# A graph network on one core: 72 instead of 76 dense blocks, seven instead of six gather steps beside each

## The chip, the cores and the metric

One NeuronCore of a Trainium2 chip runs the whole program. The metric is the device time of one execution in microseconds (us). Durations come from one execution recorded by the hardware profiler.

## The reference

A graph of 12,500 nodes and 400,000 edges (sorted by destination; low node numbers have many more incoming edges) goes through two layers, with a layer norm after each. Three times the rows of a table are summed over the edges of each node.

```python
agg = segment_sum(x[src], dst, n)                       # round 1
h   = relu(concat([x, agg / max(deg, 1)]) @ W_fc + b_fc) + x @ W_res + b_res
x   = layernorm(x + h)
# general conv, twice (rounds 2 and 3)
msg = x[src] @ Wm + bm + edge_attr @ We + be
out = segment_sum(msg, dst, n) + x @ Ws + bs            # relu between the two
x   = layernorm(x + out)
```

Since the weights can be applied ahead of the sum, each round is: a table y of 12,544 rows of 64 (65 in round 1) numbers, each split into three bf16 parts; and for each node the sum of y[src] over its edges.

## The kernel before

**Two ways of summing.** Nodes stand in 98 blocks of 128. The first 76 blocks (`END`) are *dense*: a matrix of edge counts, 128 nodes by 12,544 sources in fp16, is multiplied with the whole table, 98 matmuls of 128x192 (`dense`, L1106). The matrices are made in round 1 and stored to DRAM (`a_dram`, 3.1 MB a block); rounds 2 and 3 load them again, in two halves for each of two buffers (`a_load`, L1502). Edges of later blocks, and those that the dense lists don't take, are *gathered*: a step is a tile of 128 edges whose table rows GpSimd fetches with an indirect DMA (`g_fetch`, L1262), and three matmuls with a one-hot of the destinations (`g_multiply`, L1093); VectorE adds the result to a node block (`g_add`, L791).

**Making the matrices (round 1, `r == 0`).** A block is built in windows of 4 nodes. A step takes 128 edges, VectorE makes two one-hots from comparisons (`pairs`, L801, called in L828 to L830: one over sources' high part and the window's nodes, one over the source's lane), and TensorE multiplies them into PSUM (L1132); ACT evicts two windows at once (L1398). `REGIONS` gives for the blocks from 0, 2, 8 and 30 how many nodes one step covers (1, 1, 2, 4), and `FIRST` gives for the 256 nodes of blocks 0 and 1 how many steps each node gets: eight for the first 8 nodes, four for the next 24, three for 32, two for 192. One-hots lie in a ring of 16 steps. TensorE works on the dense product of the block before between the windows of the one being built.

**The gather steps beside.** `WITH` = 38 pairs of blocks run with `G` = 6 gather steps beside each block, 456 places. ACT converts the row numbers of six steps (`g_stage`, L1375, the tile `idx`), GpSimd issues six gathers, VectorE makes six one-hots in one operation (`g_mark`, L784, the tile `hot_g`), TensorE multiplies after the block, VectorE adds. Two sets of buffers alternate (`j`): a set is free after its product (`gsum`). In rounds 2 and 3 the second half of a list waits until half of the next dense product is done. If the list is longer than the places, a loop of `more` passes follows each round (L1162 and alike).

**What is in order where.** Each engine runs its instructions in the order written; they meet through semaphores. VectorE's queue in rounds 2 and 3 is: one-hots for the block, the reduction of the block's product (L880), its addition (L885), then the additions of the gather product. GpSimd's queue holds gathers alone in the rounds; SP's queue holds the loads or stores of matrices.

**Before and between the rounds.** A setup of some 260 us finds the edges of each step (it copies a halo of `BACK` tiles, the deepest entry of the lists, in front of each lane's edges, L1440 and L1441; shifts and comparisons over it, L532 to L564) and fetches them with GpSimd's gathers (L1213). After round 1 edge features are summed (L1172 to L1181), and the tables of rounds 2 and 3 are made ahead of each.

Of the kernel before, what the change touches and what calls it, by code (L numbers as in the profile page):

```python
# [30 lines left out]
ALU = mybir.AluOpType  # L31
ACT = mybir.ActivationFunctionType
# [3 lines left out]
P = 128  # L36
EPS = 1e-5
WD = 4
N_NODES, N_EDGES = 12500, 400000
BLOCKS = -(-N_NODES // P)  # L40

REGIONS = ((0, 1, 0), (2, 1, 1), (8, 2, 1), (30, 4, 1))
FIRST = ((8, 8), (24, 4), (32, 3), (192, 2))
END = 76
WITH = 38
WPB = P // WD
# [3 lines left out]
def runs():  # L50

    found, step = [], 0
    for n, (b, wd, k) in enumerate(REGIONS):
        end = REGIONS[n + 1][0] if n + 1 < len(REGIONS) else END
        node = b * P
        for nodes, deep in ((((end - b) * P, k),) if k else FIRST):
            found.append((node, wd, nodes // wd, deep, step))
            node += nodes
            step += nodes // wd * deep
        assert node == end * P  # L60
    return found, step

def regions():

    found, (all_runs, _) = [], runs()
    for n, (b, wd, k) in enumerate(REGIONS):
        end = REGIONS[n + 1][0] if n + 1 < len(REGIONS) else END
        inside = [run for run in all_runs if b * P <= run[0] < end * P]
        deeps = [max(run for run in inside if run[0] <= node)[3] for node in range(b * P, (b + 2) * P, WD)]  # L70
        found.append((b - REGIONS[0][0], end - b, wd, (deeps[0:WPB], deeps[WPB:2 * WPB]), inside[0][4]))
    return found
# [33 lines left out]
def gnn_program(nc, step_c, first_row, x, src, dst, edge_attr, W_fc, b_fc, W_res, b_res,  # L106
                Wm1, bm1, We1, be1, Ws1, bs1, Wm2, bm2, We2, be2, Ws2, bs2, out):
    N, D = N_NODES, x.shape[0]
    E = src.shape[0]
    assert (N, E) == (N_NODES, N_EDGES)  # L110
    T = E // P
# [7 lines left out]
    HIS = BLOCKS  # L119
    WIN = HIS * WD  # L120
    HALF = HIS // 2
    G, GW = 6, 8
    GI = WITH
# [16 lines left out]
    NB = 7  # L140
# [8 lines left out]
    CW = CG * P  # L149
    spans_of = [(s0, (REG + [(0, 0, 0, 0, CW)])[n + 1][4], wd) for n, (_, _, wd, _, s0) in enumerate(REG)]  # L150
    PIECES = 16
    HB, RING = 4, 16
    AHEAD = RING - HB + 1
    at_once = lambda wd: HB if wd == WD else 2 * HB
    YW, YW0 = BLOCKS * 3 * D // 2, BLOCKS * 3 * F1 // 2
    RINGS = RING * (P + WIN) // 2
    UNION = max(2 * CW + RINGS, 3 * CW)
    PATH = ES * P + P
    SETS = SPAD // G
# [7 lines left out]
    assert UNION >= YW >= BLOCKS * D and G * F1 <= 512 and 0 < GI <= ITERS and all(b <= 2 * GI or b - n >= 2 * GI for n, b in ((r[1], r[0] + r[1]) for r in REG)) and B0 >= 0 and DB % 2 == 0 and WPB % HB == 0  # L167
    assert all(n % 2 == 0 and s0 % P == 0 and sum(d) * WD // wd % RING == 0 for _, n, wd, ds, s0 in REG for d in ds) and HIS % 2 == 0 and (SETS - SETS % 2) * G >= T + BLOCKS - 1

    ctx = ExitStack()  # L170
    with ctx:
        def sb(name, shape, dt=F32):
            return ctx.enter_context(nc.sbuf_tensor(name, shape, dt))
# [35 lines left out]
        twofold = sb("twofold", [P, D])  # L209
        idx = sb("idx", [P, 2 * G], I32)  # L210
        hot_g = sb("hot_g", [P, 2 * G, P], F16)
        part_d = sb("part_d", [P, 2, F1])
# [24 lines left out]

        KEPT = 8 * NB
        x1_head = union[:, YW:YW + KEPT * D].rearrange("p (b d) -> p b d", d=D)
# [90 lines left out]
        trB = sb("trB", [64, P], U8)[:, :]  # L330
        trF = sb("trF", [64, P])[:, :]
        mu, root, rstd = (smallf[:, k * CG:k * CG + BLOCKS] for k in (0, 4, 8))
# [145 lines left out]
        def _(dve):  # L478
# [248 lines left out]
            for r in range(3):  # L727
# [56 lines left out]
                def g_mark(it, j):  # L784
                    dve.wait_ge(gsum[r][j], it + 1)
                    V.tensor_tensor(hot_g[:, j * G:(j + 1) * G, :],  # L786
                                    code_g[:, bass.ds((it * 2 + j) * G, G)].unsqueeze(2).to_broadcast([P, G, P]),
                                    lane16[:, 0:P].unsqueeze(1).to_broadcast([P, G, P]), ALU.is_equal)\
                        .then_inc(marked[r][j], 1)
# [20 lines left out]
                if r == 0:  # L810
# [4 lines left out]

                    for b0, blocks, wd, deeps, s0 in REG:
                        upto, pair = steps_upto(wd, deeps)
                        many = at_once(wd)
                        with dve.Fori(0, blocks // 2) as i:
                            for j in range(2):  # L820
# [3 lines left out]
                                for q in range(upto[j][0], upto[j][WPB]):  # L824
                                    n, s = q % RING, bass.ds(i * pair + (q + s0), many)
                                    if q % many == 0:

                                        dve.wait_ge(stepped, i * pair + (q + s0 + many - HB + 1))  # L828
                                        pairs(hot_c[:, n:n + many, 0:HIS * wd], twice_h, s, HIS * wd)
                                        pairs(hot_c[:, n:n + many, WIN:WIN + P], twice_l, s, P).then_inc(made, many // HB)  # L830
# [153 lines left out]
        def _(pe):  # L984
# [69 lines left out]
            for r in range(3):  # L1054
# [58 lines left out]
                if r == 0:  # L1113

                    pe.wait_ge(s_v, mark["zeros"])
                    for b0, blocks, wd, deeps, s0 in REG:
                        upto, pair = steps_upto(wd, deeps)
                        many = at_once(wd)
                        with pe.Fori(0, blocks // 2) as i:
                            for j in range(2):  # L1120
                                it = i + b0 // 2
                                for q in range(upto[j][0], upto[j][WPB]):
                                    w = max(k for k in range(WPB) if upto[j][k] <= q)
                                    c, deep = q - upto[j][w], deeps[j][w]
                                    if q % many == 0:
                                        pe.wait_ge(made, i * (pair // HB) + ((q + s0 + many) // HB))
                                    if c == 0 and w % 2 == 0:
# [66 lines left out]
        def _(pool):  # L1194
# [38 lines left out]
            for r in range(3):  # L1233
# [28 lines left out]
                def g_fetch(it, j, spread=False):  # L1262
                    pool.wait_ge(staged[r][j], it + 1)
                    pool.sem_inc(claimed, 1)
                    for k in range(G):
                        if spread and k == G // 2:

                            pool.wait_ge(a_used[1 - j][0], it + (1 + (r - 1) * ITERS + j))
                            pool.sem_inc(claimed, 1)
                        s = j * G + k  # L1270
                        pool.indirect_dma_start(msg[:, s, 0:3 * width_of[r]], None, y_tab[r], bass.IndirectOffsetOnAxis(  # L1271
                            ap=idx[:, s:s + 1], axis=0)).then_inc(gathered[r][j], 16)
# [33 lines left out]
        def _(act):  # L1306
# [28 lines left out]
            for r in range(3):  # L1335
# [39 lines left out]
                def g_stage(it, j):  # L1375
                    act.wait_ge(gsum[r][j], it + 1)
                    A.activation(idx[:, j * G:(j + 1) * G], src_g[:, bass.ds((it * 2 + j) * G, G)], ACT.Copy)\  # L1377
                        .then_inc(staged[r][j], 1)

                if r:  # L1380
# [3 lines left out]
                else:  # L1384

                    act.wait_ge(ready, 1)
                    for b0, blocks, wd, deeps, s0 in REG:
                        upto, pair = steps_upto(wd, deeps)
                        with act.Fori(0, blocks // 2) as i:
                            for j in range(2):  # L1390
# [5 lines left out]
                                for w in range(0, WPB, 2):  # L1396
                                    act.wait_ge(stepped, i * pair + (upto[j][w + 2] + s0 + AHEAD))
                                    A.activation(abuf[:, j, :].rearrange("p (h w d) -> p w h d", w=WPB, d=WD)  # L1398
                                                 [:, w:w + 2, :, :],
                                                 ps[:, w % 4:w % 4 + 2, 0:WIN].rearrange("p w (h d) -> p w h d", d=WD),  # L1400
                                                 ACT.Copy).then_inc(evacd, 2)
# [33 lines left out]
        def _(sp):  # L1435
# [55 lines left out]
            for r in range(3):  # L1491
# [26 lines left out]
                if r == 0:  # L1518

                    for b0, blocks, _, _, _ in REG:  # L1520
                        with sp.Fori(0, blocks // 2) as i:
# [66 lines left out]
```

## Time and profile before

| | us |
|---|---|
| median of three runs | 3590.77 (3587.72 to 3591.53) |
| span of the profiled execution | 3585.2 |
| setup, to about | 259 |
| round 1 | 259 to 1514 |
| edge features | 1539 to 2047 |
| round 2's dense blocks | 2151 to 2818 |
| round 3's dense blocks | 2880 to 3553 |

Busy shares of the whole span: TensorE 88%, VectorE 65%, GpSimd 56%, ACT 45%. An average over such different stages says little, so every stage is read by itself: stretches (busy time of each engine between two moments), the timeline of one engine, waits (who waited for whom, summed) and groups of instructions by line. In the views PE is TensorE's matmul, PEld its weight load, DVE VectorE, ACT ScalarE, POOL GpSimd, SP SyncE. Matmuls of one line are merged in a timeline, and their listed length has the pipeline's depth in it, so it is their starts that tell the pace.

### The profile page before, as it was taken

The numbers are of one execution on the slowest core, as the hardware profiler recorded it, in microseconds if no ns is written. First come the engines' busy times: TensorE is split into PE (matmuls) and PEld (weight loads), VectorE is DVE, ScalarE is ACT, GpSimd is POOL, SyncE is SP. The second block draws the span as 40 slices with busy tenths as digits, with TensorE's granted clock in tenths as the row PEclk, the third lists the DMA queues.
The fourth block names the chain that finished last, engine by engine and source line by source line (L and its number), as shares of the span: only waits on it lengthen the run. The fifth ranks groups of instructions, "written<-read, shape, count | busy, mean of one in ns | idle before, by whom it ended". The sixth has DMA issues, their size and how long they took to land.

```text
span 3585.2 us, 114923 instructions
## 1 busy us (share of the span) xinstructions
PE 3167.6 (88%) x39408; PEld 2958.1 (83%) x39408; DVE 2339.3 (65%) x5369; ACT 1613.7 (45%) x2096; POOL 2021.8 (56%) x2292
## 2 busy tenths in 40 slices
PE   0239999999999999889999889999999889999995
PEld 0127988888888888778888879999999889999995
DVE  8779998888888888779999682333333423333335
ACT  0123677878999999788988650000000400000000
POOL 6761234445666666534444256666666666666664
PEclk9869999999999999999999979999999999999998
DMA  3521455556666666668888429999999599999996
GB/s 92 134 18 70 167 194 198 218 213 233 238 240 251 251 238 240 245 207 247 248 246 247 147 93 400 403 402 402 402 402 403 202 354 403 402 402 402 402 402 241
DMA packets 232872, 959.10 MB, mean 268 GB/s; under 512 B 44815, under 2 KB 144285, under 8 KB 173818
## 3 DMA queue, kind: packets, MB, share of 16 engines
q1 hardware_dynamic: 186027, 884.48, 65.0%
q0 software_dynamic: 46784, 73.84, 6.8%
q8 instruction: 33, 0.54, 0.1%
q14 instruction: 28, 0.23, 0.0%
HBM read 694.75 MB, written 263.40 MB: 267 GB/s over the span
## 4 chain that ended last, share of the span: by engine, by line
PE 68%; DVE 11%; issue 8%; POOL 6%; DVEq 3%; ACT 2%; DMA 2%; SPq 0%; ACTq 0%; POOLq 0%
PE ps L1109 48%; PE ps L1132 10%; DVE union L805 5%; PE ps L1179 4%; PE ps L1101 3%; POOL abuf L1213 3%; DVE union L921 2%; ACT union L1416 1%; DVE abuf L932 1%; POOL union L1213 1%; PE ps L1069 1%; DVEq L466 1%; DVEq L932 1%; PE ps L1188 1%; POOL abuf L1255 0%
## 5 line engine op out<-in xcount | busy, mean ns | idle before, releaser
L1271 POOL DMA_INDIRECT msg<-y_tab,idx x1368 | 1531.1, 1119 | 1041.9 <-ACT idx L1377 652.0
L1109 PE MATMUL ps<-union,abuf 128*128 128x192 bf16 x14896 | 1265.3, 247 | 13.9 <-DVEq L782 10.2
L1109 PEld LDWEIGHTS ps<-union,abuf 128*128 128x128 f16 x14896 | 1226.7, 98 | 21.2 <-issue 10.6
L1398 ACT ACTIVATE abuf<-ps 128x784 f16<-128x784 f32 x1216 | 1000.7, 823 | 239.9 <-PE ps L1132 212.3
L805 DVE TENSOR_TENSOR union<-lane,union 128x1568 f16<-128x1568 f16 (+3 forms) x1440 | 949.5, 710 | 31.0 <-PE ps L1132 27.1
L1109 PE MATMUL ps<-early,abuf 128*128 128x195 bf16 x7546 | 853.4, 249 | 0.0
L1109 PEld LDWEIGHTS ps<-early,abuf 128*128 128x128 f16 x7546 | 677.1, 99 | 100.9
L1132 PE MATMUL ps<-union 128*128 128x392 f16 (+2 forms) x4288 | 689.5, 288 | 52.4 <-DVE union L805 47.1
L1377 ACT ACTIVATE idx<-src_g 128x6 int32 (+1 forms) x228 | 46.4, 205 | 1280.2 <-PE ps L1101 1277.9
L1179 PE MATMUL ps<-union 128*64 128x128 f32 x7280 | 444.4, 278 | 48.2 <-ACT union L1416 48.1
L1179 PEld LDWEIGHTS ps<-union 128*64 128x64 f32 x7280 | 394.1, 137 | 98.4 <-DVE abuf L932 79.2
L1416 ACT ACTIVATE union<-union 128x1280 f32<-128x1280 f16 x364 | 432.9, 1259 | 55.9 <-DVE union L921 53.9
L797 DVE TENSOR_TENSOR acc<-acc,ps 128x64 f32 (+1 forms) x918 | 203.7, 222 | 364.2 <-DVE acc L797 211.2
L1132 PEld LDWEIGHTS ps<-union 128*128 128x128 f16 x4288 | 362.9, 108 | 92.3 <-issue 48.3
L921 DVE TENSOR_TENSOR union<-lane,rel_e 128x640 f16<-128x640 f16 x728 | 352.5, 484 | 41.7 <-issue 40.3
L1291 POOL TENSOR_TENSOR rel_e<-early,base_e 128x10 f16 x728 | 208.4, 305 | 287.5 <-DVE union L921 271.1
L880 DVE TENSOR_REDUCE part_d<-ps 128x64 f32<-128x192 f32 x152 | 54.4, 358 | 459.2 <-PE ps L1109 459.2
L786 DVE TENSOR_TENSOR hot_g<-code_g,lane 128x768 f16<-128x768 f16 x228 | 218.0, 956 | 70.2 <-DVE acc L797 69.2
L932 DVE TENSOR_TENSOR abuf<-abuf,ps 128x128 f32 x728 | 203.5, 280 | 1.8 <-PE ps L1179 1.1
L1101 PE MATMUL ps<-msg,hot_g 128*128 128x64 bf16 (+1 forms) x4104 | 167.2, 194 | 5.5 <-DMA msg<-y_tab,idx 5.5
L1101 PEld LDWEIGHTS ps<-msg,hot_g 128*128 128x128 f16 x4104 | 157.0, 98 | 6.0 <-DMA msg<-y_tab,idx 6.0
L854 DVE TENSOR_TENSOR acc<-acc,ps 128x65 f32 x456 | 99.5, 218 | 56.8 <-DVE acc L854 37.9
(229 smaller groups left out, 1241.4 us busy)
## 6 DMA issues: line engine op xcount, KB each, us to landing
abuf<-a_dram SPq DMA_DIRECT2D x304, 1568.0 KB
a_dram<-abuf SPq DMA_DIRECT2D x76, 3136.0 KB
union<-in_edge_attr_dram SPq DMA_DIRECT2D x728, 160.0 KB, 2.9
msg<-y_tab,idx POOLq DMA_INDIRECT x1368
y_tab<-union SPq DMA_DIRECT2D x28, 336.0 KB, 2.2
abuf<-in_x_dram SPq DMA_DIRECT2D x28, 224.0 KB, 3.4
y_tab<-early SPq DMA_DIRECT2D x7, 682.5 KB, 5.5
out_dram<-union SPq DMA_DIRECT2D x2, 800.0 KB, 3.5
```

The source lines that it names most:

```text
L786: V.tensor_tensor(hot_g[:, j * G:(j + 1) * G, :], code_g[:, bass.ds((it * 2 + j) * G, G)].unsqueeze(2).to_broadcast([P, G, P]), lane16[:, ...
L805: return V.tensor_tensor(to.rearrange("p s (c u) -> p s c u", u=2), lanes.unsqueeze(1).to_broadcast([P, n, width // 2, 2]), codes[:, which ...
L921: marks = V.tensor_tensor(mark_e[:, h, :, :].rearrange("p j (c u) -> p j c u", u=2), lane16[:, 0:P].rearrange("p (c u) -> p c u", u=2).uns ...
L932: V.tensor_tensor(to, to, ps[:, b, 0:P], ALU.add).then_inc(e_add, 1)
L1101: last = nc.tensor.matmul(tile_ps(r, j, k), hot_g[:, s, :], msg[:, s, c * width_of[r]:(c + 1) * width_of[r]], start=c == 0, stop=c == 2)
L1109: last = nc.tensor.matmul(ps[:, bank, 0:3 * width_of[r]], abuf[:, buffer, hi * P:(hi + 1) * P], ycols[r][:, hi, :], start=hi == 0, stop=hi ...
L1132: nc.tensor.matmul(ps[:, w % 4, 0:WIN].rearrange("p (h d) -> p h d", d=WD)[:, :, d0:d0 + wd], hot_c[:, n, WIN:WIN + P], hot_c[:, n, 0:HIS ...
L1179: last = nc.tensor.matmul(ps[half:half + D, h, 0:P], feats[:, h, j * D:(j + 1) * D], hot_e[:, h, j, :], start=j < 2, stop=j >= EG - 2)
L1271: pool.indirect_dma_start(msg[:, s, 0:3 * width_of[r]], None, y_tab[r], bass.IndirectOffsetOnAxis(ap=idx[:, s:s + 1], axis=0)).then_inc(ga ...
L1291: nc.gpsimd.tensor_tensor(rel_e[:, h, :, :], flat(dst_e[:, bass.ds(grp[h], 1), :]).unsqueeze(2) .to_broadcast([P, EG, 2]), base_e[:, bass. ...
L1398: A.activation(abuf[:, j, :].rearrange("p (h w d) -> p w h d", w=WPB, d=WD) [:, w:w + 2, :, :], ps[:, w % 4:w % 4 + 2, 0:WIN].rearrange("p ...
L1416: A.activation(hot_e[:, h:h + 2, :, :], mark_e[:, h:h + 2, :, :], ACT.Copy)\
```

## The change

Dense blocks end at 72 instead of 76, with seven gather steps beside each (504 places instead of 456). The lists of blocks 0 and 1 become 14 steps for the first 4 nodes, six for 20, three for 32, two for 200. A region's list begins at a multiple of 128 columns now (`s0`), and the count of steps before it is kept apart for the semaphores (`e0`). In rounds 2 and 3 ACT converts the destination codes of a list as well, to fp32 in a new tile `codes`, and VectorE makes each step's one-hot by itself, comparing the lanes with one number per lane; it waits for ACT's copy, and GpSimd's wait counts in twos. The scratch tile `trF` moves into `part_d`.

```diff
-FIRST = ((8, 8), (24, 4), (32, 3), (192, 2))
-END = 76
-WITH = 38
+FIRST = ((4, 14), (20, 6), (32, 3), (200, 2))
+END = 72
+WITH = 36
...
         node = b * P
+        step = -(-step // P) * P
...
-    G, GW = 6, 8
+    G, GW = 7, 8
...
+        codes = sb("codes", [P, 2 * G])
...
-        trF = sb("trF", [64, P])[:, :]
+        trF = part_d[0:64, :, :].rearrange("p j d -> p (j d)")[:, 0:P]
...
                 def g_mark(it, j):
                     dve.wait_ge(gsum[r][j], it + 1)
+                    if r:
+                        dve.wait_ge(staged[r][j], it * 2 + 2)
+                        for s in range(j * G, (j + 1) * G):
+                            last = V.tensor_scalar(hot_g[:, s, :], lane16[:, 0:P], codes[:, s:s + 1], None, ALU.is_equal)
+                        last.then_inc(marked[r][j], 1)
+                        return
...
-                                        dve.wait_ge(stepped, i * pair + (q + s0 + many - HB + 1))
+                                        dve.wait_ge(stepped, i * pair + (q + e0 + many - HB + 1))
...
                 def g_fetch(it, j, spread=False):
-                    pool.wait_ge(staged[r][j], it + 1)
+                    pool.wait_ge(staged[r][j], it * 2 + 1 if r else it + 1)
...
                     A.activation(idx[:, j * G:(j + 1) * G], src_g[:, bass.ds((it * 2 + j) * G, G)], ACT.Copy)\
                         .then_inc(staged[r][j], 1)
+                    if r:
+                        A.activation(codes[:, j * G:(j + 1) * G], code_g[:, bass.ds((it * 2 + j) * G, G)], ACT.Copy)\
+                            .then_inc(staged[r][j], 1)
```

## Rows read from the trace of the kernel before

**Rows 1.** Stretches: length, busy time (instructions) by engine, clock, DMA share, GB/s.

```profile
2151.00:2818.00 667.00, 663.83 (x8795) 660.26 (x8793) 216.14 (x676) 15.36 (x74) 453.58 (x456) 0.99 1.00 398
...
498.70:831.50 332.80, 305.45 (x3603) 282.67 (x3601) 295.72 (x500) 265.01 (x341) 151.96 (x121) 1.00 0.55 212
902.30:1475.50 573.20, 573.20 (x5922) 485.45 (x5921) 503.59 (x1000) 530.72 (x680) 357.50 (x240) 1.00 0.63 245
```

**Rows 2.** Timeline of TensorE, rounds 2 and 3: start, length, instructions, idle before.

```profile
2166.76 0.74 PE L1101 MATMUL ps<-msg,hot_g 128*128 128x64 bf16 x18 [0.30 <-DMA msg<-y_tab,idx]
...
2626.50 0.72 PE L1101 MATMUL ps<-msg,hot_g 128*128 128x64 bf16 x18
...
2635.22 0.73 PE L1101 MATMUL ps<-msg,hot_g 128*128 128x64 bf16 x18
2635.79 8.29 PE L1109 MATMUL ps<-union,abuf 128*128 128x192 bf16 x98
...
2818.13 0.72 PE L1101 MATMUL ps<-msg,hot_g 128*128 128x64 bf16 x18
...
2894.78 1.14 PE L1101 MATMUL ps<-msg,hot_g 128*128 128x64 bf16 x18 [5.25 <-DMA msg<-y_tab,idx]
...
3548.23 0.72 PE L1101 MATMUL ps<-msg,hot_g 128*128 128x64 bf16 x18
```

**Rows 3.** DMA, 2300 to 2500: packets, MB, share of 16 engines; gathers issued.

```profile
q0 software_dynamic: 4419, 6.79, 9.5%
...
msg<-y_tab,idx POOLq DMA_INDIRECT x139
```

**Rows 4.** Timeline of GpSimd and VectorE in round 2.

```profile
2160.82 0.95 POOL L1271 DMA_INDIRECT msg<-y_tab,idx  x1 [0.30 <-issue]
...
2302.13 0.96 DVE L786 TENSOR_TENSOR hot_g<-code_g,lane 128x768 f16<-128x768 f16 x1 [0.72 <-DVE acc L797]
...
2302.36 1.55 POOL L1271 DMA_INDIRECT msg<-y_tab,idx  x1 [0.30 <-issue]
...
2314.54 0.94 POOL L1271 DMA_INDIRECT msg<-y_tab,idx  x1 [1.28 <-issue]
```

**Rows 5.** The same two engines' timelines in the setup.

```profile
114.02 2.17 POOL L1213 DMA_INDIRECT union<-both_dram,gidx  x1 [0.30 <-issue]
...
114.98 1.09 DVE L611 TENSOR_SCALAR acc<-code_g,tiles 125x3328 f16<-125x3328 f16 x1
...
119.12 0.94 POOL L1213 DMA_INDIRECT union<-both_dram,gidx  x1 [0.30 <-issue]
...
119.23 0.42 DVE L623 TENSOR_SCALAR acc<-code_g,tiles 125x768 f16<-125x768 f16 x1
```

**Rows 6.** Groups, 902 to 1475: count, busy us, mean ns, idle before.

```profile
L854 DVE TENSOR_TENSOR acc<-acc,ps 128x65 f32 x240 | 52.5, 219 | 33.1 <-DVE acc L854 21.4 <-DVE acc L848 11.6
L786 DVE TENSOR_TENSOR hot_g<-code_g,lane 128x768 f16<-128x768 f16 x40 | 38.0, 951 | 0.0
```

**Rows 7.** Waits, 902 to 1475: us in total, times, longest.

```profile
DVE part_d L842 <- PE ps L1101: 21.8, 40, 0.7
...
DVE union L805 <- PE ps L1132: 13.5, 40, 0.3
```

**Rows 8.** Waits, 498 to 831.

```profile
DVE union L805 <- PE ps L1132: 10.5, 40, 0.3
DVE part_d L842 <- issue: 9.0, 20, 0.5
```

**Rows 9.** Groups, 268 to 358.

```profile
L805 DVE TENSOR_TENSOR union<-lane,union 128x1024 f16<-128x1024 f16 x78 | 53.3, 683 | 0.0
...
L805 DVE TENSOR_TENSOR union<-lane,union 128x784 f16<-128x784 f16 x78 | 43.8, 561 | 0.1
```

**Rows 10.** DMA, 0 to 20.

```profile
DMA packets 733, 4.45 MB, mean 223 GB/s; under 512 B 264, under 2 KB 264, under 8 KB 388
```

**Rows 11.** Timeline of VectorE in the setup.

```profile
22.45 2.36 DVE L532 CAST union<-abuf 125x4224 int16<-125x4224 int32 x1
```

More of the change, by code:

```diff
@@ L64, in regions @@
 def regions():
-    found, (all_runs, _) = [], runs()
+    found, (all_runs, _), before = [], runs(), 0
     for n, (b, wd, k) in enumerate(REGIONS):
@@ L70, in regions @@
         deeps = [max(run for run in inside if run[0] <= node)[3] for node in range(b * P, (b + 2) * P, WD)]
-        found.append((b - REGIONS[0][0], end - b, wd, (deeps[0:WPB], deeps[WPB:2 * WPB]), inside[0][4]))
+        found.append((b - REGIONS[0][0], end - b, wd, (deeps[0:WPB], deeps[WPB:2 * WPB]), inside[0][4], before))
+        before += sum(windows * deep for _, _, windows, deep, _ in inside)
     return found
@@ L149, in gnn_program @@
     CW = CG * P
-    spans_of = [(s0, (REG + [(0, 0, 0, 0, CW)])[n + 1][4], wd) for n, (_, _, wd, _, s0) in enumerate(REG)]
+    spans_of = [(s0, (REG + [(0, 0, 0, 0, CW)])[n + 1][4], wd) for n, (_, _, wd, _, s0, _) in enumerate(REG)]
     PIECES = 16
@@ L156, in gnn_program @@
     RINGS = RING * (P + WIN) // 2
-    UNION = max(2 * CW + RINGS, 3 * CW)
+    KEPT = 8 * NB
+    UNION = max(2 * CW + RINGS, 3 * CW, YW + KEPT * D)
     PATH = ES * P + P
@@ L167, in gnn_program @@
     assert UNION >= YW >= BLOCKS * D and G * F1 <= 512 and 0 < GI <= ITERS and all(b <= 2 * GI or b - n >= 2 * GI for n, b in ((r[1], r[0] + r[1]) for r in REG)) and B0 >= 0 and DB % 2 == 0 and WPB % HB == 0
-    assert all(n % 2 == 0 and s0 % P == 0 and sum(d) * WD // wd % RING == 0 for _, n, wd, ds, s0 in REG for d in ds) and HIS % 2 == 0 and (SETS - SETS % 2) * G >= T + BLOCKS - 1
+    assert all(n % 2 == 0 and s0 % P == 0 and sum(d) * WD // wd % RING == 0 for _, n, wd, ds, s0, _ in REG for d in ds) and HIS % 2 == 0 and (SETS - SETS % 2) * G >= T + BLOCKS - 1
     ctx = ExitStack()
@@ L236, in gnn_program @@
         hot_c = union[:, 2 * CW:2 * CW + RINGS].bitcast(F16).rearrange("p (s c) -> p s c", s=RING)
-        KEPT = 8 * NB
         x1_head = union[:, YW:YW + KEPT * D].rearrange("p (b d) -> p b d", d=D)
@@ L813, in _ @@
                     step(V.memset(ps[:, 7, :], 0.0), "zeros")
-                    for b0, blocks, wd, deeps, s0 in REG:
+                    for b0, blocks, wd, deeps, s0, e0 in REG:
                         upto, pair = steps_upto(wd, deeps)
@@ L1115, in _ @@
                     pe.wait_ge(s_v, mark["zeros"])
-                    for b0, blocks, wd, deeps, s0 in REG:
+                    for b0, blocks, wd, deeps, s0, e0 in REG:
                         upto, pair = steps_upto(wd, deeps)
@@ L1125, in _ @@
                                     if q % many == 0:
-                                        pe.wait_ge(made, i * (pair // HB) + ((q + s0 + many) // HB))
+                                        pe.wait_ge(made, i * (pair // HB) + ((q + e0 + many) // HB))
                                     if c == 0 and w % 2 == 0:
@@ L1386, in _ @@
                     act.wait_ge(ready, 1)
-                    for b0, blocks, wd, deeps, s0 in REG:
+                    for b0, blocks, wd, deeps, s0, e0 in REG:
                         upto, pair = steps_upto(wd, deeps)
@@ L1396, in _ @@
                                 for w in range(0, WPB, 2):
-                                    act.wait_ge(stepped, i * pair + (upto[j][w + 2] + s0 + AHEAD))
+                                    act.wait_ge(stepped, i * pair + (upto[j][w + 2] + e0 + AHEAD))
                                     A.activation(abuf[:, j, :].rearrange("p (h w d) -> p w h d", w=WPB, d=WD)
@@ L1518, in _ @@
                 if r == 0:
-                    for b0, blocks, _, _, _ in REG:
+                    for b0, blocks, _, _, _, _ in REG:
                         with sp.Fori(0, blocks // 2) as i:
```

## The prediction

> **What bounds the kernel now.** First the stretches by stage [rows 1]: in round 2 (2151 to 2818) TensorE is busy 663.8 of 667 us, but the DMA engines are busy throughout too, at 398 GB/s; two limits lie on top of each other. TensorE's timeline tells which one is ahead [rows 2]: a block with its gather product returns every 8.72 us late in the round (2626.50 to 2635.22), while the whole round's 75 intervals from first to last product (2166.76 to 2818.13, 651.4 us) average 8.685, so early ones are shorter (if half go at 8.72, the others go at 8.65). That is a TensorE that first outruns the transfers, uses up what was loaded ahead, and then goes at their pace: 8.72 is the DMA limit, about 8.65 TensorE's. Round 3 is alike (653.5 us). Third, GpSimd's timeline [rows 4]: a gather takes 0.94 us and 0.30 lies between two, so six need 7.5 of the 8.7 us. It waits for its index list in between, and nobody waits for it except at a round's start, where the first product stands at 2166.76 though the sixth gather was issued at 2160.82.
>
> In round 1, blocks 30 and up (40 of them from 902.3 to 1475.5, 14.33 us each) have TensorE busy 573.2 of 573.2 us [rows 1], with VectorE at 503.6. Blocks 8 to 29 (20 from 498.7 to 831.5, 16.64 us each) have TensorE at 305.4 and VectorE at 295.7 of 332.8 us: there they pass the ring of one-hots back and forth and each waits for the other. Blocks 0 to 7 go by VectorE's one-hots.
>
> **Does the work fit the loops?** A fallback loop of further gathers runs after each round if the list is longer than the steps beside the blocks. I counted the list on the reference's edges by the kernel's own rule (a tile is listed, once for each block it spans, if one of its edges is beyond the lists' depth or at a node past the last dense block): 436 of 456 places before, 496 of 504 after. Each round issues 504 gathers instead of 456, with no loop behind. Without the deeper first lists it would have been 514.
>
> **The change part by part**, in us.
>
> *Four blocks fewer in round 1:* 4 x 14.33 = -57.3.
>
> *The seventh step in round 1.* For TensorE three matmuls: eighteen take 0.57 (2635.22 to 2635.79) [rows 2], so 0.095 a block. For VectorE a sixth more one-hot (0.951 / 6 = 0.16) and one more addition (0.219, and 33.1 / 240 = 0.14 of waiting) [rows 6], together 0.52. GpSimd has room: it is busy 357.5 of 573.2 us in the last region [rows 1], and a sixth more is 417. In the 42 blocks from 30 on, VectorE stands idle for TensorE (21.8 + 13.5) / 40 = 0.88 a block [rows 7]; that hides 0.52, and I take 0.095 plus 0.025 for imperfect cover: +5.0. Its ends are 4.0, and 21.8 if the cover is gone. In blocks 8 to 29 VectorE's waits are (10.5 + 9.0) / 20 = 0.98 a block [rows 8], but TensorE waits for VectorE as well, so little of it is free: between 0.1 and 0.52 a block, and I take 0.4, near the upper end because of that coupling: +8.8. In blocks 2 to 7, VectorE-bound, the whole 0.52: +3.1.
>
> *The deeper first lists.* 4 x 14 + 20 x 6 + 32 x 3 + 200 x 2 = 672 steps in blocks 0 and 1 instead of 640, four more groups of eight, each 0.683 + 0.561 of one-hots [rows 9]: 5.0, and two times 0.52: +6.0 (4 to 9; the uneven windows may empty the ring).
>
> *Setup.* The copied halo is 14 tiles instead of 8, 6 x 128 x 4 bytes on 125 lanes = 384 KB more ahead of the first use; at 223 GB/s [rows 10] 1.7. The cast over it is 4992 instead of 4224 columns, 2.36 x 768 / 4224 = 0.4 [rows 11], and the shifts under which GpSimd's setup gathers lie are longer too: +2.5 (1 to 4). Starting each region's list at a multiple of 128 only moves columns, and the scratch tile that now lies in another is written and read ahead of the rounds: nothing.
>
> *The one-hots of rounds 2 and 3.* One VectorE operation over 768 elements becomes seven over 128, each with one number per lane that ACT copies. ACT is idle there, and sends GpSimd's list before it copies the codes. VectorE's new wait for the codes has the round's reductions and additions queued behind it and TensorE behind those; but the copy follows a product that lies a block earlier than the place in VectorE's queue, so it is long done. VectorE has 450 us to spare in the round. What is open is what seven short operations do to the gathers, below.
>
> *Rounds 2 and 3, the block.* Three engines must each get through a block. TensorE: 8.65 + 0.095 = about 8.75. DMA: 139 gathers took 9.5% of the 16 engines over 200 us [rows 3], 0.137 each; 8.72 + 0.135 = 8.855. GpSimd: 7 x (0.94 + 0.30) = 8.73 by rounded rows, back to back (no extra between two lists at the round's start), plus a pause of about 1 us that comes once in some 108 gathers (2314.54, idle 1.28) [rows 4], 0.06 a block, plus 0.05 where a gather meets the addition of two SBUF operands, plus what the one-hots cost. The old one-hot stretched the gather that it met, 1.55 instead of 0.94 (2302.36, one-hot at 2302.13) [rows 4]. For the new ones the nearest rows are in the setup [rows 5]: the gather at 114.02 met two comparisons of 1.09 and took 2.17, but the one at 119.12 met comparisons of 0.42 and 0.56 and took 0.94. So a hold lasts to the end of an operation, and short ones cost little: 0 to 0.4 a block; I take 0.13, nearer the second row, since operations over 128 elements are shorter still. Sum 8.97, the latest of the three. **So the rounds change hands from TensorE and DMA to GpSimd's queue.** As the first product of a round already waits for its gathers, no reserve delays that: every later one follows at GpSimd's rate. 71 intervals x 8.97 = 636.9, against 651.4 and 653.5: -14.5 and -16.6, together -31.1. A list of seven is also issued 1.25 later at each round's start, where it is waited for: +2.5. At the ends of the three rounds one more addition stands alone: +1.2.
>
> The rest (edge features, tables between the rounds, the end) is not touched.
>
> **Sum:** -57.3 + 5.0 + 8.8 + 3.1 + 6.0 + 2.5 - 31.1 + 2.5 + 1.2 = -59.3. The profiled span of 3585.2 becomes 3525.9; the median shown lies 5.6 above it, so 3590.8 - 59.3 = 3531.5.
>
> **The rivals.**
>
> *DMA sets the rounds.* The seven short operations slip between gathers, GpSimd keeps under 8.855. For: the setup gather at 119.12. Against: GpSimd's own 8.73 leaves only 0.12 for everything else. 2 x 71 x (8.855 - 8.97) = -16.3, so 3515.
>
> *VectorE takes over round 1.* Its added 0.52 a block isn't covered from block 8 on: 42 x (0.52 - 0.12) + 22 x 0.12 = +19.4, so 3551. For: it is busy 88% already and its additions are a chain. Against: the 0.88 of idle time.
>
> *The one-hots hold the gathers: slower than before.* If each of the seven keeps GpSimd out for its own length (about 0.2, by 0.42 for 768 elements and a fixed part), a block takes 8.84 + 1.4 = 10.24: 142 x 1.27 = +180, so 3711. It decides from 8.97 + 59.3 / 142 = 9.39 a block, which is 0.55 of holding a block. For: the gather at 114.02 was held through two comparisons. [...] Against: GpSimd is held at a few points of a gather, not all along it (0.94 at 119.12), so most of the 1.4 meets nothing.
>
> *The list doesn't fit,* if my count is off: one pass of the loop behind each round is two lists and a landing, 2 x 8.73 + 5.0 = 22, three times 67, so 3598.
>
> **How the numbers follow.** Forecast 0.56, DMA 0.20, VectorE 0.12, held gathers 0.10 (0.03 of it so mild that it ends within 0.2%), list 0.02 (half of it within). A measurement of this kernel can tell about 0.2%, 7 us. Faster 0.56 + 0.20 + 0.12 = 0.88, same 0.04, slower 0.08. The range takes the low ends of every term with DMA-bound rounds (1 + 4 + 1.2 + 2.2 + 4 + 1.2 + 2.5 - 57.3 - 47.5 = -88.7, 3502) and, above, the VectorE case with rounds at 9.15 (-8.8 - 5.6 = -14.4, 3576). It leaves out the last two rivals.
>
> **What would show it.** Right: 1512 gathers of lists and no loop behind; a block of 14.4 to 14.5 in round 1's last region; in rounds 2 and 3 GpSimd's idle time before a list gone, 0.30 between all gathers, TensorE waiting a few tenths in each block for gathers, and a DMA share just under full. Wrong: TensorE's intervals at 8.85 with GpSimd still waiting for ACT (DMA won), gathers above 1.04 on average (the one-hots hold them), VectorE without waits in round 1 (it took over).

## The result, and the profile after

The changed kernel takes 3640.03 us (median of 4 runs, 3636.75 to 3643.39) against 3589.80 for the kernel before: 1.0138 times as long, 95% interval 1.0124 to 1.0153. The forecast was 3531, faster. Runs of one kernel can differ by some 18 us, because one short stage (the fold, below) runs at a granted TensorE clock of 1.00 or of about 0.52; the profiled execution of the kernel before had it at 1.00, that of the changed one at 0.52.

The profiled span is 3641.6 us, 56.4 more than before. Where they come from, by the starts of the stages on TensorE's timeline (of the terms for the round starts and the rounds' ends, each part is put where it belongs):

| part | predicted | measured |
|---|---|---|
| setup, up to the first adjacency matmul | +2.5 | +4.5 |
| round 1, to its last dense block (-57.3 + 5.0 + 8.8 + 3.1 + 6.0) | -34.4 | -29.7 |
| round 1's end to the edge features | +0.4 | +1.4 |
| **edge features** | 0 | **+67.6** |
| **fold behind them** | 0 | **+18.7** |
| to round 2's first product | +1.3 | +3.6 |
| round 2, first to last product | -14.5 | -4.7 |
| to round 3's first product | +1.7 | +1.9 |
| round 3 | -16.6 | -7.5 |
| end | +0.4 | +0.6 |
| sum | -59.3 | +56.4 |

All but two rows have the sign that was forecast; the two that don't belong to a stage that the change leaves as it was. Stretches of edge features and fold (length, busy time and instructions of TensorE, its weight loads, VectorE, ACT and GpSimd, TensorE's granted clock, DMA share, GB/s), the kernel before:

```profile
1539.00:2025.30 486.30, 444.45 (x7281) 394.14 (x7281) 441.56 (x1456) 431.87 (x364) 205.87 (x720) 0.99 0.80 244
2025.30:2047.10 21.80, 21.80 (x195) 21.80 (x196) 0.97 (x2) 6.70 (x12) 0.00 (x0) 1.00 0.00 1
```

and the changed kernel:

```profile
1515.40:2069.00 553.60, 467.73 (x7281) 421.11 (x7281) 447.49 (x1455) 436.66 (x363) 202.54 (x718) 0.94 0.73 215
2069.00:2109.50 40.50, 40.50 (x196) 40.50 (x196) 0.99 (x2) 6.98 (x12) 0.00 (x0) 0.52 0.00 1
```

The same instructions in a stretch 67 us longer. VectorE's busy time is nearly the same (447.49 for 441.56 us), so 61 us of the 67 are idle time of VectorE; TensorE's busy time is 23 us longer, in a stretch in which its granted clock averages 0.94 for 0.99. The fold is 196 matmuls back to back, at a granted clock of 1.00 before (21.8 us) and 0.52 after (40.5 us).

Who waits in the edge features shows the place. Waits of the stretch (in all, how often, the longest), before and then after; "issue" is time in which the engine waited for nothing that the profile shows:

```profile
DVE union L921 <- issue: 40.3, 51, 1.3
```
```profile
DVE union L930 <- issue: 82.2, 51, 4.9
PEld ps L1188 <- DVE abuf L941: 121.8, 134, 8.5
ACT union L1428 <- DVE union L930: 111.2, 85, 5.1
DVE abuf L941 <- PE ps L1188: 10.4, 20, 0.6
DVE abuf L941 <- issue: 8.6, 34, 0.3
```

The others wait for VectorE, and VectorE for the most part waits for nothing visible. Its loop runs 13 turns of 56 tiles; once a turn, where the loop goes back, stands one long pause: 1.25 us before, 4.0 to 4.9 after (start, length, operation, idle before). The wait in which these pauses stand grew by 42 us (40.3 to 82.2); the rest of the 67 is in small pieces inside the turns, among them VectorE's own two waits at L941 (0.6 and 1.1 us before).

```profile
1611.99 0.28 DVE L932 TENSOR_TENSOR abuf<-abuf,ps 128x128 f32 x1
1613.52 0.49 DVE L921 TENSOR_TENSOR union<-lane,rel_e 128x640 f16<-128x640 f16 x1 [1.25 <-issue]
```
```profile
1593.54 0.28 DVE L941 TENSOR_TENSOR abuf<-abuf,ps 128x128 f32 x1
1597.91 0.49 DVE L930 TENSOR_TENSOR union<-lane,rel_e 128x640 f16<-128x640 f16 x1 [4.10 <-issue]
```

A row at the end of the DMA view of the same stretches (queue, packets, MB, share) says what VectorE may be waiting for: its instructions. Before and after:

```profile
q14 instruction: 4, 0.03, 0.0%
```
```profile
q14 instruction: 65, 0.53, 0.4%
```

61 more packets over 12 returns of the loop, five a return, 8 KB each. One of each five starts about a microsecond into the long pause and the next about when it ends; the same row for 1637 to 1642, with the pause that ends at 1641.4:

```profile
q14 instruction: 2, 0.02, 0.9%
```

The loop's code is the same; but the change adds 60 instructions ahead of it in VectorE's program: 52 for the seventh addition in each loop of round 1 and in the fallback loop, 8 for the deeper first lists. Counted in the order in which the program lists them, without those that only wait for or raise a semaphore, the loop's 312 instructions lay at places 1058 to 1370 and lie now at 1118 to 1430. With the semaphore instructions the trace has 340 in a turn; the shift is 60 either way.

Rounds 2 and 3 answer to [rows 2, 4]. TensorE's first and last products of both rounds, 72 in each (start, length, idle before):

```profile
2232.84 0.58 PE L1110 MATMUL ps<-msg,hot_g 128*128 128x64 bf16 x13 [3.17 <-DMA msg<-y_tab,idx]
...
2879.55 0.59 PE L1110 MATMUL ps<-msg,hot_g 128*128 128x64 bf16 x14
...
2958.13 0.61 PE L1110 MATMUL ps<-msg,hot_g 128*128 128x64 bf16 x8 [5.07 <-DMA msg<-y_tab,idx]
...
3604.03 0.56 PE L1110 MATMUL ps<-msg,hot_g 128*128 128x64 bf16 x13
```

71 intervals of 9.109 and 9.097 us, where 8.97 was forecast. They are not alike: in round 2 59 of 71 are 8.74 to 8.82, and most of the rest stand in clumps of two or three, 16 blocks apart. GpSimd and TensorE at the first clump:

```profile
2358.51 0.95 POOL L1280 DMA_INDIRECT msg<-y_tab,idx  x1 [0.30 <-ACT idx L1386]
2359.76 0.95 POOL L1280 DMA_INDIRECT msg<-y_tab,idx  x1 [0.30 <-issue]
2366.19 0.95 POOL L1280 DMA_INDIRECT msg<-y_tab,idx  x1 [5.49 <-issue]
...
2366.03 0.82 PE L1110 MATMUL ps<-msg,hot_g 128*128 128x64 bf16 x21
2366.70 8.26 PE L1118 MATMUL ps<-union,abuf 128*128 128x192 bf16 x98
2378.41 1.30 PE L1110 MATMUL ps<-msg,hot_g 128*128 128x64 bf16 x21 [3.45 <-DMA msg<-y_tab,idx]
2379.52 10.58 PE L1118 MATMUL ps<-union,abuf 128*128 128x192 bf16 x98
2389.94 0.82 PE L1110 MATMUL ps<-msg,hot_g 128*128 128x64 bf16 x21
```

GpSimd stands still for 5.49 us between two gathers of one list. TensorE then waits 3.45 for that list, and the block behind takes 10.58 instead of 8.26, because the clock has fallen (in the row of this stretch it is the third number from the right, 0.50):

```profile
2378.40:2381.00 2.60, 2.59 (x31) 2.51 (x32) 0.45 (x3) 0.31 (x2) 1.89 (x2) 0.50 1.01 395
```

So two intervals of 12.38 and 11.53, about 6.4 us lost here, and about 5 to 6 at each of four such places a round. In the kernel before the pause of this kind was 1.28 [rows 4], and nobody waited for it.

### The profile page after: what moved, and what is told of

The parts are those of the page before. It is cut to its first block, busy times and chain, and to the rows that moved or that the text cites. A ratio compares the mean times of both kernels' runs of the same rounds, so it can differ in the third digit from the quotient of the medians.

```text
span 3641.6 us, 114539 instructions
## 1 busy us (share of the span) xinstructions
PE 3127.8 (86%) x38568; PEld 2925.0 (80%) x38568; DVE 2379.0 (65%) x6286; ACT 1579.8 (43%) x2164; POOL 2104.5 (58%) x2436
## 4 chain that ended last, share of the span: by engine, by line
PE 48%; POOL 16%; issue 15%; DVE 11%; DMA 6%; DVEq 3%; ACT 2%; ACTq 0%; POOLq 0%; SPq 0%
PE ps L1118 30%; POOL msg L1280 10%; PE ps L1141 7%; DVE union L814 5%; PE ps L1188 5%; DMA msg<-y_tab,idx 4%; POOL abuf L1222 3%; PE ps L1110 3%; DVE union L930 2%; ACT union L1428 1%; DVE abuf L941 1%; POOL union L1222 1%; PE ps L1197 1%; DVEq L469 1%; PE ps L1078 1%
## 5 line engine op out<-in xcount | busy, mean ns | idle before, releaser
L1280 POOL DMA_INDIRECT msg<-y_tab,idx x1512 | 1614.4, 1068 | 921.5 <-issue 456.4
L1118 PE MATMUL ps<-union,abuf 128*128 128x192 bf16 x14112 | 1210.7, 248 | 14.7 <-DVEq L785 10.2
L1118 PEld LDWEIGHTS ps<-union,abuf 128*128 128x128 f16 x14112 | 1177.4, 99 | 18.5 <-issue 10.6
L1410 ACT ACTIVATE abuf<-ps 128x784 f16<-128x784 f32 x1152 | 949.1, 824 | 262.1 <-PE ps L1141 237.2
L814 DVE TENSOR_TENSOR union<-lane,union 128x1568 f16<-128x1568 f16 (+1 forms) x1384 | 911.9, 710 | 8.4 <-PE ps L1141 4.7
L1118 PE MATMUL ps<-early,abuf 128*128 128x195 bf16 x7154 | 809.3, 249 | 0.0
L1118 PEld LDWEIGHTS ps<-early,abuf 128*128 128x128 f16 x7154 | 641.9, 99 | 92.1
L1141 PE MATMUL ps<-union 128*128 128x98 f16 (+2 forms) x4192 | 661.3, 287 | 57.4 <-DVE union L814 56.3
L1386 ACT ACTIVATE idx<-src_g 128x7 int32 (+1 forms) x216 | 44.4, 205 | 1258.8 <-PE ps L1110 1248.1
L930 DVE TENSOR_TENSOR union<-lane,rel_e 128x640 f16<-128x640 f16 x728 | 351.7, 483 | 83.7 <-issue 82.2
L792 DVE TENSOR_SCALAR hot_g<-lane,codes 128x128 f16<-128x128 f16 x1008 | 182.3, 270 | 67.5 <-DVE acc L806 65.0
L941 DVE TENSOR_TENSOR abuf<-abuf,ps 128x128 f32 x728 | 203.3, 279 | 21.6 <-PE ps L1188 10.4
```

Source lines behind the costliest of these rows:

```text
L814: return V.tensor_tensor(to.rearrange("p s (c u) -> p s c u", u=2), lanes.unsqueeze(1).to_broadcast([P, n, width // 2, 2]), codes[:, which ...
L930: marks = V.tensor_tensor(mark_e[:, h, :, :].rearrange("p j (c u) -> p j c u", u=2), lane16[:, 0:P].rearrange("p (c u) -> p c u", u=2).uns ...
L941: V.tensor_tensor(to, to, ps[:, b, 0:P], ALU.add).then_inc(e_add, 1)
L1118: last = nc.tensor.matmul(ps[:, bank, 0:3 * width_of[r]], abuf[:, buffer, hi * P:(hi + 1) * P], ycols[r][:, hi, :], start=hi == 0, stop=hi ...
L1141: nc.tensor.matmul(ps[:, w % 4, 0:WIN].rearrange("p (h d) -> p h d", d=WD)[:, :, d0:d0 + wd], hot_c[:, n, WIN:WIN + P], hot_c[:, n, 0:HIS ...
```

## The experiments

Theory 1: the edge features are slower because VectorE fetches its loop's code anew in each turn, and does so because of where the loop lies. The rival: something that the loop works with (buffers moved, clock, transfers).

**68 instructions that are never run.** In VectorE's branch for leftover gathers, which this input doesn't take:

```diff
                 with dve.If(more > 0):
+                    if r == 0:
+                        for _ in range(68):
+                            V.memset(part_d[0:1, 0, 0:1], 0.0)
```

> The changed kernel with 68 one-element memsets written into VectorE's branch for leftover gathers of the first round. That branch isn't taken with this input, so nothing more is executed; VectorE's instructions behind it lie 68 places later, its loop of the edge features among them: places 1186 to 1498 in place of 1118 to 1430 (before the change 1058 to 1370), the same place as before the change if places are counted in blocks of 128. Theory 1 (VectorE fetches part of that loop's code anew in each of its turns, because of where the loop lies): the pause of 4.0 to 4.9 us per turn falls to about 1.3 us, the instruction queue's packets in the stretch fall from 65 to under 10, edge features plus fold take 508 us in place of 594, the whole about 3640 - 86 = 3554 us. Rival (the loop is slower by what it waits for: the new buffer layout, the one-hots, the transfers, or the clock): nothing changes, 3640 us.

Measured: 3556.38 us, 0.9889 of the kernel before (0.9848 to 0.9930), 84 under the changed kernel. The edge features:

```profile
1517.10:2003.60 486.50, 444.48 (x7280) 394.27 (x7280) 441.31 (x1454) 431.56 (x363) 205.87 (x718) 1.00 0.81 243
```

with the instruction queue's packets and VectorE's waits in the same stretch:

```profile
q14 instruction: 5, 0.04, 0.0%
```
```profile
DVE union L933 <- issue: 40.8, 51, 1.3
```

The fold behind it takes 21.9 us at 1.00. All as before the change, by code that doesn't run. The rival falls.

**The same done to the kernel before,** 60 memsets in the same branch.

> The kernel before with 60 one-element memsets in the same branch, not taken either: VectorE's loop of the edge features moves from places 1058 to 1370 to 1118 to 1430, where it lies in the changed kernel. Theory 1: the pause per turn rises from 1.3 to 4 to 5 us, edge features plus fold from 508 to about 594 us, the whole to 3590 + 86 = 3676 us. Rival: no change, 3590 us.

Measured: 3666.35 us, 1.0179 times the kernel before (1.0136 to 1.0223). Its edge features and fold, and the instruction queue in the first:

```profile
1540.80:2093.10 552.30, 467.09 (x7280) 419.81 (x7280) 447.62 (x1455) 436.54 (x363) 201.87 (x718) 0.94 0.72 215
2093.10:2132.30 39.20, 39.20 (x195) 39.20 (x196) 1.00 (x2) 6.95 (x12) 0.00 (x0) 0.53 0.00 0
```
```profile
q14 instruction: 64, 0.52, 0.3%
```

So 60 instructions that never run reproduce the whole loss in a kernel with nothing else changed. Of the 86 us that were expected, the runs part what belongs to the code from what doesn't: its four runs are 3656.47, 3659.41, 3673.30 and 3674.28, those of the kernel before beside it 3584.96 to 3591.42 and 3604.66 to 3610.23. Group against group that is 66 to 70 us, the edge features alone; the other 17 or 18 fit the fold's clock, which falls in some runs of either kernel (mean granted clock 0.958 and 0.959 against 0.953, and 0.966 to 0.968 against 0.961 and 0.962).

**132 instead of 68.**

> The changed kernel with 132 memsets in the branch that isn't taken, in place of 68: VectorE's loop of the edge features lies 132 places later than in the changed kernel, that is 4 places further within a block of 128, but half a block of 256 further. [...] Theory 1 with blocks of 256 places: as with 68, about 3556 us.

Measured: 3630.42 us (one run), 546.9 us for the edge features and 65 packets:

```profile
1514.30:2061.20 546.90, 466.16 (x7281) 419.44 (x7281) 448.00 (x1455) 437.93 (x363) 206.63 (x718) 0.94 0.73 217
```
```profile
q14 instruction: 65, 0.53, 0.3%
```

**Rounds 2 and 3.** Theory 2 on GpSimd's pause was that it waits for the first gather of its loop's current turn. With three iterations in the body of that loop:

```diff
-                with pool.Fori(0, GI) as i:
-                    for j in range(2):
-                        g_fetch(i, j, r > 0)
+                at_a_time = 3 if r else 1
+                with pool.Fori(0, GI, at_a_time) as i:
+                    for m in range(at_a_time):
+                        for j in range(2):
+                            g_fetch(i + m, j, r > 0)
```

> The changed kernel with GpSimd's loop of rounds 2 and 3 written with three iterations (42 gathers) in its body in place of one (14). The same gathers in the same order behind the same waits. Theory 2 (every so many gathers GpSimd pauses until the first gather of the loop's current turn has landed, and in the changed kernel the pause falls right behind that gather): the first pause of a round stays behind gather 113, but that is then the 30th of its turn, whose first gather landed 30 us earlier, so the pause falls from 5.5 to about 1.2 us; the next ones come every 84 gathers, five a round; a round loses about 19 us of its 646, the whole is about 3640 - 38 = 3602 us. Rival (the queue of gathers is full, and it waits for what is outstanding, wherever the loop stands): pauses of 5.5 us every 112 or 113 gathers, 3640 us.

> Both of the edits together: the changed kernel with 68 memsets in the branch that isn't taken, and 42 gathers in the body of GpSimd's loop in rounds 2 and 3. Theories 1 and 2 together: 3640 - 86 - 38 = about 3516 us, which would be 2% under the kernel before. Theory 1 alone 3554, theory 2 alone 3602, neither 3640 us.

Measured: 3637.37 us, and with the memsets 3572.97 (runs at 3555 to 3556 and at 3573 to 3576). Neither differs from its partner without the longer body by more than the fold's clock, and in both every pause stands where it stood, behind gathers 113, 225, 337 and 449 of a round, 5.5 us long:

```profile
2362.17 0.94 POOL L1280 DMA_INDIRECT msg<-y_tab,idx  x1 [5.53 <-issue]
```

Theory 2 falls: the loop's turn has nothing to do with it.

**Half of the dense loads left out,** to see whether the transfers set the blocks or the pause:

```diff
-                    sp.dma_start(abuf[:, j, u * HALF * P:(u + 1) * HALF * P],
+                    end = (u + 1) * HALF * P if u == 0 or isinstance(it, int) else HALF * P + P
+                    sp.dma_start(abuf[:, j, u * HALF * P:end],
```

> The changed kernel with the 68 memsets that aren't run (3556 us). It leaves out work: in rounds 2 and 3, from the third dense block on, of the second half of each block of the adjacency matrix one column tile of 49 is loaded, so the DMA engines carry about half. Theory 3 (GpSimd's gathers set the pace of rounds 2 and 3, and its pause every 112 gathers is the landing of the gather just issued, which is late because the DMA engines are full): the blocks stay at 8.75 us, the pauses fall from 5.5 to the 1.6 us of round 1, a round falls by 4 x 4 = 16 us, the whole to about 3524 us. Rival A (the pause has a length of its own): pauses of 5.5 us, 3556 us. Rival B (the transfers set the pace): blocks well under 8.75 us and a total under 3500 us.

Measured: 3526.38 us (one run). Round 2, and the first pause in it:

```profile
2148.00:2778.00 630.00, 623.98 (x8447) 623.16 (x8448) 241.49 (x1134) 21.46 (x140) 465.97 (x493) 1.00 0.65 219
```
```profile
2277.33 0.94 POOL L1283 DMA_INDIRECT msg<-y_tab,idx  x1 [2.08 <-issue]
```

The undisturbed blocks keep their 8.74 to 8.82 us with the DMA engines at 0.65, so the transfers don't set them (rival B falls). The pauses shrink to 2.0 to 2.9 us and the rounds from 645 to 630 and 631.5: the pause's length goes with the load on the DMA engines (5.5 us at a share of 0.99 in round 2 of the changed kernel, 2.0 to 2.9 at 0.65; rival A falls), and what shrank is worth 14 to 15 us a round. Theory 3 comes near in its sizes; that the pause is the landing of the gather just issued isn't shown by that.

**Four more gathers ahead of each loop,** to see whether the place in the list sets the pause's length:

```diff
+                if r:
+                    pool.wait_ge(staged[r][0], 1)
+                    for k in range(4):
+                        pool.indirect_dma_start(msg[:, G + k, 0:3 * D], None, y_tab[r], bass.IndirectOffsetOnAxis(
+                            ap=idx[:, 0:1], axis=0)).then_inc(extra, 16)
```

> The changed kernel with the 68 memsets that aren't run (3556 us), and at the start of rounds 2 and 3 four more gathers (of rows already gathered, into slots not in use), which shift the place of the pauses against the lists of seven. Theory 3, with the pause waiting for the first gather of the list that is being issued: the first pause of these rounds still comes behind 113 gathers, which is now behind the list's fourth, 3.7 us later than that first gather, and lasts 1.2 to 2 us; what is freed reaches to the start of that list, so the second comes 109 gathers later, again behind a list's first gather, and lasts 5.5 us, as those behind it. Two pauses of eight are shorter by about 4 us, the eight gathers cost 10: 3555 to 3565 us. Rival (the pause is 5.5 us wherever it falls in a list, every 112 gathers): eight pauses of 5.5 us, 3566 us.

Measured: 3578.35 us (one run, its fold 39.5 us at 0.53). The four are issued in one row with the lists, and yet each round's first pause comes behind its 113th gather of lists, 5.5 us long, and the others every 112. The four were not counted; so the place in the list couldn't be varied, and the test doesn't decide. Its theory fails in the count.

**GpSimd's loop cut into five** of at most 112 gathers.

```diff
+                cuts = (0, 8, 16, 24, 30, GI) if r else (0, GI)
+                for first, end in zip(cuts, cuts[1:]):
+                    with pool.Fori(0, end - first) as i:
+                        for j in range(2):
+                            g_fetch(i + first, j, r > 0)
```

> The changed kernel with the 68 memsets that aren't run (3556 us), and GpSimd's loop of rounds 2 and 3 cut into five loops one behind the other, of 8, 8, 8, 6 and 6 iterations, so that none issues more than 112 gathers. Theory 4 (what is counted up to the pause starts anew with each loop: it starts anew with each round, and four gathers put in ahead of a loop were not counted in it): no pause of 5.5 us is left, a round falls from 645 to about 71 x 8.76 + 2 = 625 us, the whole to about 3516 us, unless a new loop's first instructions take as long to fetch. Rival (the count runs on across loops while gathers are outstanding): pauses as before at gathers 113, 225, 337 and 449 of a round, 3556 us.

Measured: 3556.20 us, 0.9872 of the kernel before (0.9829 to 0.9915), no different from the kernel with the memsets alone; eight pauses of 5.4 to 5.9 us behind the same gathers. Theory 4 falls. What counts the gathers, and why the pause is 1.28 us with lists of six (every 108 gathers, behind a list's fifth) and 5.5 with lists of seven (every 112, behind a list's first) under DMA engines about as full (shares of 1.00 and 0.99 in round 2, 398 and 383 GB/s), stays open.

**The one-hots,** put back in the changed kernel with the memsets, and put alone into the kernel before:

```diff
                     dve.wait_ge(gsum[r][j], it + 1)
-                    if r:
-                        dve.wait_ge(staged[r][j], it * 2 + 2)
-                        for s in range(j * G, (j + 1) * G):
-                            last = V.tensor_scalar(hot_g[:, s, :], lane16[:, 0:P], codes[:, s:s + 1], None, ALU.is_equal)
-                        last.then_inc(marked[r][j], 1)
-                        return
```

> The changed kernel with the 68 memsets that aren't run (3556 us), and in rounds 2 and 3 with the one-hots of a gather step again written by one TENSOR_TENSOR instead of seven TENSOR_SCALAR; the copy of the codes goes too. Theory (a block of rounds 2 and 3 is now GpSimd's seven gathers, 7 x 1.247 = 8.73 us, and the old instruction stretches the gathers under it): before the change the gathers of rounds 2 and 3 took 0.993 and 0.981 us on average where an undisturbed one takes 0.944, about 0.3 us a block of six; with seven that is 0.3 to 0.4 us, on 142 intervals 43 to 57 us: about 3606 us. Rival (the stretch lies in GpSimd's idle time, as before the change): 3556 us.

> The kernel before with the one-hots of rounds 2 and 3 alone changed: six TENSOR_SCALAR per gather step, with the copy of the codes; six steps, 76 blocks and the lists stay. VectorE's code ahead of its loop of the edge features is not touched. Theory: GpSimd idles 0.9 to 1.4 us in every block of rounds 2 and 3 of the kernel before, so that it doesn't set the pace there; shorter gathers only lengthen the idle time: 3590 us. Rival (the stretched gathers sat on the path): 152 blocks x 0.25 us less, about 3552 us.

Measured: put back 3588.48 us, 32 more than 3556.38. The gathers of round 2 (count, busy, mean ns, idle before) with the old one-hots, and with the new:

```profile
L1277 POOL DMA_INDIRECT msg<-y_tab,idx x493 | 496.8, 1008 | 173.0 <-issue 161.4 <-ACT idx L1383 5.8 <-PE ps L1115 5.8
```
```profile
L1283 POOL DMA_INDIRECT msg<-y_tab,idx x493 | 466.0, 945 | 173.8 <-issue 168.3 <-PE ps L1121 3.9 <-ACT codes L1392 1.5
```

31 us of stretching in GpSimd, and the round is 28.7 longer (71 x 9.492 against 71 x 9.088); in round 3 fewer gathers are met (mean 962) and 6 us are lost. Put alone into the kernel before: 3590.39 against 3590.86 us, ratio 0.9996 (0.9979 to 1.0014). There the gathers get as short (996 to 944 ns), and GpSimd waits the difference away (first the kernel before, then with the edit):

```profile
L1271 POOL DMA_INDIRECT msg<-y_tab,idx x444 | 442.2, 996 | 199.0 <-issue 119.8 <-ACT idx L1377 79.2
```
```profile
L1278 POOL DMA_INDIRECT msg<-y_tab,idx x447 | 421.8, 944 | 222.6 <-issue 119.8 <-ACT codes L1387 102.6 <-PE ps L1116 0.3
```

The same edit is worth nothing that can be measured with six gathers and 32 us with seven.

## Why the prediction was wrong

**The step that failed is one sentence: "The rest (edge features, tables between the rounds, the end) is not touched."** No line of it is, but its code moved by 60 places, and 86.3 of the 115.7 us between forecast and result come from the stages that it puts at nothing: 67.6 in the edge features, which three shifts by code that doesn't run show to be the moved code, and 18.7 in the fold. That the fold's clock falls is not settled as an effect of the change: it fell too in the run with four gathers ahead, whose edge features were as fast as before. The sign of the result doesn't hang on it, since the edge features alone outweigh the 30 us that the other stages gained.

**Round 1** gained 29.7 for 34.4. Blocks 8 to 29 go at 16.90 us, +0.27, where +0.4 was taken. From block 30 on the average is 14.68, +0.35 a block in place of 0.12: of the 42 blocks every second one takes 14.43 and every other 14.92. VectorE still waits, as in [rows 7], and TensorE now waits for gathers in every second block (waits, 909 to 1464):

```profile
DVE part_d L851 <- PE ps L1110: 23.1, 37, 0.9
...
PE ps L1110 <- DMA msg<-y_tab,idx: 6.3, 19, 0.4
```

GpSimd's timeline of one such list, and the product that needs it:

```profile
1303.28 1.58 POOL L1280 DMA_INDIRECT msg<-y_tab,idx  x1 [3.72 <-ACT idx L1386]
...
1314.30 0.95 POOL L1280 DMA_INDIRECT msg<-y_tab,idx  x1 [0.30 <-issue]
...
1316.83 0.85 PE L1110 MATMUL ps<-msg,hot_g 128*128 128x65 bf16 x21 [0.31 <-DMA msg<-y_tab,idx]
```

The list is released by the product before (1301.92, through ACT's copy), its seven gathers take 12 us under VectorE's one-hots, and the last lands 1.6 us after its issue ends: the chain from product to product is 14.9 us. "GpSimd has room: it is busy 357.5 of 573.2" read a share of busy time where the chain of one list had to be laid out; with six gathers a list took 10.4 to 10.5 us, about 1.5 less, and TensorE had no such wait. The deeper lists, in one sum with the first blocks, were near: the first reduction comes 9.9 later (285.43 to 295.37), of which 4.5 are the setup and 5.4 the lists (6.0).

**Setup** +4.5 for +2.5: the wider cast starts 2.1 later and is 0.4 longer, as worked out; the other 2 come up later, on the stretch of shifts, comparisons and GpSimd's gathers, where the forecast had 0.4; what causes them wasn't traced.

**Rounds 2 and 3** gained 12.2 for 31.1. The block was put at 8.97 as GpSimd's: 8.73, and 0.13 + 0.05 for one-hots and additions, 0.06 for the pause. The two small terms did not come: gathers take 945 ns on average, undisturbed. The old one-hot had stretched them (1008 ns on average with it put back), the new ones don't; the seven operations are 270 ns each, the old one 1.09 us. The 0.05 for the addition of two SBUF operands is in none of the rows read from the kernel before, whose trace has one such gather (2167.07, 0.99 us); in the changed kernel the 136 gathers that met this addition (L894) in rounds 2 and 3 took 948 ns on average, five of them 987 to 998. So an undisturbed block is 8.76 (mean of the 59), TensorE's 8.75 of the forecast, with GpSimd's 8.73 (seven times 1.247; the 0.94 and 0.30 as printed would give 8.68) so close beneath that it can't make up for a pause. And the pause, taken over at its size of 1.28 us, was 5.5: with TensorE's drop to a granted clock of 0.50 behind it, about 5 to 6 us four times a round. Together with the first, longer interval of a round that is 0.35 a block in place of 0.06. The DMA limit of 8.855 did not bind: blocks of 8.76 stand with full loads, and with half of them they stay the same. Whether it would bind without the pauses, in which the transfers go on (409 GB/s from 2360 to 2366, in the first), no run shows; nor was it tested that the late 8.72 of the kernel before is the transfers.

**Of the rivals** none is what happened. That the gathers are held is refuted (945 ns); DMA-bound rounds, VectorE as the bound of round 1 and a list that doesn't fit (1512 gathers, no loop behind) likewise. With the loop's code 128 places on from where it was, the changed kernel takes 3556 us, inside the range of 3502 to 3576 and 25 over the forecast; nearly all of that is rounds 2 and 3 (19) and round 1 (5).

## What to carry to other kernels

An edit ahead of a long loop on the same engine moves the loop's code, and the loop can then begin to be fetched anew in each turn (here one of 340 instructions, 5 us a turn); compare the instruction queue's packets stage by stage (here 4 before and 65 after), also of stages that were not edited, and if they rise, move the code by instructions in a branch that isn't taken. For an engine with work in lists, lay out one list from its release to its landing beside the block; its busy share (here 357.5 of 573.2 us) doesn't tell whether it fits. And an operation that stretches another engine's work is worth removing only where that engine has no idle time left: here nothing measurable with six gathers a block, 32 us with seven.

## What the runs showed of the hardware

- VectorE's loop of 340 instructions a turn (312 in the count of places) costs 5 packets of 8 KB and about 5 us a turn when it lies badly (places 1118 or 1250: 64 or 65 packets in the stretch, pauses of 3.9 to 4.9 us at a return), and no packet at a return when it lies well (1058 or 1186: 4 or 5 packets, pauses of 1.2 to 1.3 us).
- 196 matmuls back to back took 21.8 or 21.9 us, or 39.2 to 40.5, in profiles of kernels that have this stretch alike, at a granted clock of 1.00 or 0.52 to 0.53; with the same edge features ahead of them, both occur (21.9 us at 1.00 with the 68 memsets alone, 39.5 at 0.53 with the four gathers ahead as well).
- In the changed kernel TensorE's granted clock fell from 1.00 (2360 to 2366) to 0.50 (2378.4 to 2381) over an idle time of 3.45 us, and the 98 matmuls of the next block took 10.58 us instead of 8.26.
- In rounds 2 and 3 GpSimd pauses behind 113 gathers of a round's lists and then every 112 (lists of seven) or 108 (of six): for 1.2 to 1.3 us with six, for 5.4 to 5.9 with seven (5.2 to 6.6 with the old one-hots), for 2.0 to 2.9 with seven and half of the dense loads; neither the length of the loop's body, nor a new loop, nor four gathers ahead moved the place.
